# Graph attention, one core: each unit's s1 row spread into PSUM by a TensorE matmul of three bfloat16 parts

## The chip, the cores and the metric

The kernel runs on one core of a Trainium2 chip. The metric is device time in microseconds (us), lower is better; the time before is the median of three runs.

## The reference

One graph attention layer with eight heads, a residual and a layer norm, for 8 graphs of 2048 nodes with 512 features:

```
h  = einsum('bnf,hfo->bhno', x, W)            # 8 heads, 64 features each
s1 = einsum('bhno,ho->bhn', h, a1);  s2 = einsum('bhno,ho->bhn', h, a2)
e  = leaky_relu(s1[..., :, None] + s2[..., None, :], 0.2)
attn = softmax(where(adj > 0, e, -9e15), axis=-1)
out = layernorm(x + concat_heads(attn @ h))
```

## The kernel before

exp(leaky_relu(s1 + s2)) is a product of two factors wherever the sign of s1 + s2 is known, so the attention is worked out as two matmuls with masks of zeros and ones: m_pos holds the edges on which s1_i + s2_j is positive, m_neg the other edges. No exponential of a 2048 x 2048 matrix is taken.

**Work and its units.** A batch is one graph. Its 2048 rows i are cut into KB = 4 blocks of BLK = 512, and each block is done for H = 8 heads, so a batch has UNITS = 32 units (block, head), and the kernel 256. The columns j are cut into JC = 16 chunks of 128, eight to each half ("quad", QUADS = 2).

**A unit on the engines.**
- SyncE (`load_s1`, L261) loads the unit's row of 512 values s1 from DRAM, where `store_s1` put it, into all 128 partitions of `s1_bc`, two buffers deep. Ahead of it, it waits until ScalarE and VectorE have done with the buffer. It also loads adjacency pieces (`load_piece`), transposes them (`turn_piece`), loads x tiles and stores finished blocks, all in one queue, in the order of the program.
- ScalarE (`compare`, L505) copies the row from `s1_bc` into PSUM bank 5 (L510) and then makes 13 of the 16 chunks of `step` (L519), each a steep Relu of s1_i + s2_j that reads the PSUM bank. Around it stand, in its queue, the cuts of adjacency pieces to one byte (`cut_piece`, L487) and the copies of transposed x tiles out of PSUM (`copy_xT`, L493).
- VectorE (L707) makes the other three chunks from `s1_bc` in SBUF, then `m_pos` = step AND mask (`make_pos`, L722) and `m_neg` = m_pos XOR mask (`make_neg`, L731), two instructions each. It waits for ScalarE's half of `step`, and for TensorE to be done with the buffer. Then it takes the finished unit out of PSUM (`take_unit`, L576 to L581). Layer norm and a batch's preparation go between.
- TensorE, for each of four blocks of 128 rows, adds a matmul of a tiny term (L448) and 32 matmuls of 65 columns with m_pos (L454, L455) into one PSUM bank, and then in the same way 32 for m_neg (L475, L476) into another: 260 matmuls to a unit, each with its weight load. Between the two halves it may do a step for the next batch: transpose an x tile (`turn_x`, L368; 16 of the 32 units), sum x (`turn_x_sum`, unit 24), the scores (`sum_scores`, unit 25), `turn_scores` and `mean_h` (unit 27).
- GpSimd divides, adds the residual, sums x, and takes a maximum over partitions once a batch (L862).

**Order.** Every engine runs the same loop over batches. ScalarE and VectorE make the masks of unit u+1 while TensorE multiplies unit u; the masks have two buffers, so VectorE's m_pos of unit u+1 needs the first half of TensorE's unit u-1 to be over. At the head of a batch the hidden features h of all 16 chunks are multiplied (L429, in the three PSUM banks H_BANKS in turn), and VectorE and GpSimd split them into high and low parts (`split_chunk`, L693 to L698): this is called the batch head below, and the 32 units the unit stage. At the end of a batch VectorE prepares the next: `score_maxima` in unit 28, `exponents` in unit 29, `no_edge_start` and `no_edge_part` in unit 30, and `turn_s2` (L665, L666) in unit 31, which ScalarE's first compare of the next batch waits for.

PSUM banks: 0 to 3 hold the sums of two units, 4 the mean and the sum of x, 5 the s1 row, 6 and 7 x tiles and scores; h uses 7, 4 and 6.

Of the kernel before, what the change touches and what calls it, by code (L numbers as in the profile page):

```python
# [60 lines left out]
def gat_kernel(nc, x, adj, W, a1, a2, out):  # L61
# [16 lines left out]
    H_BANKS = (7, 4, 6)  # L78
# [9 lines left out]
    with ExitStack() as ctx:  # L88
# [18 lines left out]
        BANK_MEAN = 4  # L107
        BANK_SUM = 4
        BANK_S1 = 5
        BANK_X = 6  # L110

# [18 lines left out]
        sT = sb("sT", [P, BLK], F32)  # L130
        s_col = sb("s_col", [P, JC, 2 * H], F32)
# [88 lines left out]
        s1_copied = sem("s1_copied")  # L220
# [39 lines left out]
        def _(sp):  # L260
            def load_s1(u, slot):  # L261

                sp.wait_ge(step_act, at(step_act, QUADS * (u - 1)))
                sp.sem_inc(waited[sp.engine], 1)
                sp.wait_ge(step_dve, at(step_dve, u - 1))
                sp.dma_start(s1_bc[slot][:], s1_rows[bass.ds(u, 1), :].rearrange("a n -> (a n)").partition_broadcast(P)
                             ).then_inc(s1_loaded[slot], 16)
# [95 lines left out]
        def _(pe):  # L363
# [8 lines left out]
            def turn_x_sum(n):  # L372
                if type(n) is int:
                    pe.wait_ge(x_added, at(x_added, JC))
                else:
                    pe.wait_ge(x_summed, 16 * JC * n)
                for fc in range(FC):
                    mm = pe.matmul(ps[:, BANK_SUM, fc:fc + 1], x_sum[:, fc * P:(fc + 1) * P], ones[:, 0:1],
                                   start=True, stop=True)
                mm.then_inc(x_sum_turned, 1)  # L380
# [8 lines left out]

            def turn_scores(n):  # L390
                pe.wait_ge(sT_copied, n + 1)
                for t in range(IT):
                    mm = pe.transpose(ps[:, BANK_X + 1, t * P:(t + 1) * P], sT[:, t * P:(t + 1) * P], ident[:])
                mm.then_inc(s_turned, 1)
# [21 lines left out]
            sum_scores(0)  # L416
            mean_h(0)
            turn_scores(0)

            with nc.Fori(0, B, engines=[pe.engine], hint_back_edge=True) as b:  # L420
                for jc in range(JC):
                    if jc == 0:
                        pe.wait_ge(s_col_copied, b + 1)
                    if jc == 1:
                        pe.wait_ge(tiny_step, 6 * b + 1)
                    if jc >= 3:
                        pe.wait_ge(hi_d_made, b * JC + jc - 2)
                    for fc in range(FC):
                        mm = pe.matmul(ps[:, H_BANKS[jc % 3], :], xT[:, fc, jc * P:(jc + 1) * P], W_sb[:, fc, :],  # L429
                                       start=(fc == 0), stop=(fc == FC - 1))  # L430
                    mm.then_inc(h_summed, 1)
                for k in range(KB):
                    g = b * KB + k
                    for h in range(H):
# [22 lines left out]
                        if unit == 0:  # L457
                            pe.wait_ge(lo_made, at(lo_made, 2 * JC * (b + 1)))
                        if unit and unit in TILE_UNIT:
                            t = TILE_UNIT.index(unit)  # L460
                            turn_x(JC * (b + 1) + t, t % 2, (b + 1) * (JC // 2) + t // 2)
# [19 lines left out]
        def _(act):  # L481
# [12 lines left out]

            def copy_scores(n):
                act.wait_ge(sT_summed, n + 1)
                nc.scalar.activation(sT[:], ps[:, BANK_X, :], ACT.Copy).then_inc(sT_copied, 1)

# [6 lines left out]
            def compare(u, h, nth):  # L505
                act.wait_ge(s1_loaded[h % 2], 16 * (nth + 1))
                act.sem_inc(waited[act.engine], 1)

                act.wait_ge(step_act, at(step_act, QUADS * u))
                nc.scalar.activation(ps[:, BANK_S1, :], s1_bc[h % 2][:], ACT.Copy).then_inc(s1_copied, 1)  # L510
                act.wait_ge(s1_copied, u + 1)
                act.sem_inc(waited[act.engine], 1)
                for qd in range(QUADS):
                    act.wait_ge(pos_made, at(pos_made, QUADS * (u - 1) + qd + 1))
                    act.sem_inc(waited[act.engine], 1)
                    for c in range(JQ):
                        if c not in DVE_SLOTS.get(qd, ()):
                            j = qd * JQ + c
                            ins = nc.scalar.activation(chunk(step[qd], c, 0, BLK), ps[:, BANK_S1, :], ACT.Relu,  # L519
                                                       bias=s2_steep[:, j, h:h + 1], scale=STEEP, saturate=False)  # L520
# [10 lines left out]
            exponentials(0)  # L531
            act.wait_ge(s2_turned, 1)
            compare(0, 0, 0)

            with nc.Fori(0, B, engines=[act.engine], hint_back_edge=True) as b:
                for k in range(KB):
                    g = b * KB + k
                    for h in range(H):
# [8 lines left out]
                        if unit == STURN_UNIT:  # L547
                            copy_scores(b + 1)
                        if unit < UNITS - 1:
                            compare(u + 1, (h + 1) % H, g * (H // 2) + (h + 1) // 2)  # L550
                        else:
                            exponentials(b + 1)
                            with act.If(b < B - 1):
                                act.wait_ge(s2_turned, b + 2)
                                act.sem_inc(waited[act.engine], 1)
                                compare(u + 1, 0, (g + 1) * (H // 2))
# [5 lines left out]
        def _(dve):  # L562
# [51 lines left out]
            def score_maxima(n):  # L614
# [7 lines left out]
                V.tensor_reduce(stat[:, H:H + 1], xmax[:], AX.X, ALU.max).then_inc(stat_made, 1)  # L622

# [122 lines left out]
            V.memset(ones_bf[:], 1.0).then_inc(ones_bf_made, 1)  # L746
            V.memset(wa[:], 0.0)
# [27 lines left out]
            score_maxima(0)  # L775
            turn_s2(0)
# [6 lines left out]
            with nc.Fori(0, B, engines=[dve.engine], hint_back_edge=True) as b:  # L783
# [13 lines left out]
                for k in range(KB):  # L797
                    g = b * KB + k
                    for h in range(H):
# [17 lines left out]
                        if unit == STAT_UNIT:  # L817
                            score_maxima(b + 1)
                        if unit == STAT_UNIT + 1:
# [147 lines left out]
```

## Time and profile before

| | |
|---|---|
| median of 3 runs | 3147.84 us (3135.4 to 3163.03) |
| the profiled execution | 3138.42 us |
| its span, first to last instruction | 3136.7 us |
| mean granted TensorE clock | 0.967 of full speed |

The terms below are read in the profiled execution, whose span leaves 1.7 us of its own time outside. It lies 9.4 us (0.3%) under the median of the runs, so a difference in it is carried over to the median as it stands. In the views, PE is TensorE's matmuls, PEld its weight loads, DVE VectorE, ACT ScalarE, POOL GpSimd and SP SyncE. "issue" names idle time in which an engine waited for nothing that the profile shows.

### The profile page before, as it was taken

To read this page: it belongs to the slowest core of one execution; us is meant where nothing else is said; L and a number is where in the kernel's file an instruction comes from. 1 tells how busy PE (TensorE), PEld (TensorE's weight loads), DVE (VectorE), ACT (ScalarE), POOL (GpSimd) and SP (SyncE) were. 2 spreads that over 40 slices of the span, in tenths; PEclk is the share of its full clock that TensorE was granted. 3 is DMA by queue.
4 is the path that set the end of the run, shared out by engine and by line. 5 is a ranking of instruction groups with operands and counts; after the bars stand their busy time and mean duration, and the time that the engine had idled before them with its cause. 6 is when DMAs were issued, how large, how long until landed. Compare 5 with 4: busy or idle time off the path is not lost.

```text
span 3136.7 us, 158793 instructions
## 1 busy us (share of the span) xinstructions
PE 2744.1 (87%) x68636; PEld 2398.0 (76%) x68636; DVE 2522.8 (80%) x3954; ACT 2419.3 (77%) x4029; POOL 827.5 (26%) x1011
## 2 busy tenths in 40 slices
PE   4898889998898898988989889998898888988886
PEld 2498876988678885888858888498884888758886
DVE  4888878887887878888788787888877877788876
ACT  2499973999658996599856998479973989739994
POOL 2522115111341113312142111521215111161211
PEclk9999999999999999999999999999999999999998
DMA  5357643576526655277442765437644556345753
GB/s 162 93 116 161 141 100 100 123 164 131 130 71 136 150 130 136 63 157 157 111 118 70 159 155 122 98 88 165 150 108 115 112 143 156 90 112 115 165 135 94
DMA packets 281338, 392.28 MB, mean 125 GB/s; under 512 B 161856, under 2 KB 161856, under 8 KB 280672
## 3 DMA queue, kind: packets, MB, share of 16 engines
q1 hardware_dynamic: 253536, 315.24, 39.9%
q0 software_dynamic: 27136, 67.12, 12.7%
q8 instruction: 545, 8.93, 1.2%
q14 instruction: 121, 0.99, 0.2%
HBM read 313.52 MB, written 34.14 MB: 111 GB/s over the span
## 4 chain that ended last, share of the span: by engine, by line
PE 67%; issue 13%; DVE 10%; ACT 7%; DMA 1%; SPq 1%; POOL 0%; DVEq 0%; ACTq 0%; POOLq 0%
PE ps L475 14%; PE ps L476 14%; PE ps L455 13%; PE ps L454 13%; PE ps L429 8%; ACT step L519 7%; PE ps L368 2%; DVE m_neg L731 1%; DVE y L603 1%; PE ps L386 1%; PE ps L399 1%; DVE prod L695 1%; PE ps L448 1%; DVE prod_d L698 1%; DVE m_pos L722 1%
## 5 line engine op out<-in xcount | busy, mean ns | idle before, releaser
L519 ACT ACTIVATE step<-ps,s_steep 128x512 fp8e4<-128x512 f32 x3328 | 1954.1, 726 | 289.7 <-DVE m_pos L722 246.9
L455 PE MATMUL ps<-b_lo,m_pos 128*128 128x65 f16 x16384 | 1094.3, 195 | 96.4 <-issue 95.4
L454 PE MATMUL ps<-b_hi,m_pos 128*128 128x65 f16 x16384 | 1093.7, 195 | 54.4 <-issue 36.5
L475 PE MATMUL ps<-d_hi,m_neg 128*128 128x65 f16 x16384 | 1071.9, 195 | 67.0 <-issue 61.2
L455 PEld LDWEIGHTS ps<-b_lo,m_pos 128*128 128x128 fp8e5 x16384 | 1052.3, 98 | 101.3 <-issue 101.0
L475 PEld LDWEIGHTS ps<-d_hi,m_neg 128*128 128x128 fp8e5 x16384 | 1043.6, 99 | 98.5 <-issue 97.9
L476 PE MATMUL ps<-d_lo,m_neg 128*128 128x65 f16 x16384 | 1072.7, 195 | 42.3 <-issue 42.1
L454 PEld LDWEIGHTS ps<-b_hi,m_pos 128*128 128x128 fp8e5 x16384 | 1052.5, 98 | 66.3 <-issue 66.1
L476 PEld LDWEIGHTS ps<-d_lo,m_neg 128*128 128x128 fp8e5 x16384 | 1039.1, 99 | 34.9 <-issue 33.3
L722 DVE TENSOR_TENSOR m_pos<-step,maskT 128x1024 uint32<-128x1024 uint32 x512 | 623.8, 1242 | 163.4 <-ACT step L519 130.6
L731 DVE TENSOR_TENSOR m_neg<-m_pos,maskT 128x1024 uint32<-128x1024 uint32 x512 | 602.8, 1217 | 0.0
L429 PE MATMUL ps<-W_sb,xT 128*128 128x512 f32 x1024 | 464.1, 615 | 61.5 <-DVE prod_d L698 54.7
L871 POOL TENSOR_TENSOR den_scaled<-den_inv,bound 128x4 f32<-128x4 f32 x256 | 74.9, 292 | 1592.0 <-DVE den_inv L581 1533.9
L429 PEld LDWEIGHTS ps<-W_sb,xT 128*128 128x128 f32 x1024 | 200.8, 198 | 319.3 <-issue 240.6
L707 DVE TENSOR_SCALAR step<-s_bc,s_neg 128x512 fp8e5<-128x512 f32 x768 | 391.1, 565 | 12.4 <-DVE s_neg L666 3.6
L487 ACT ACTIVATE adj_cut<-adj_in 128x1024 fp8e4<-128x1024 int32 x264 | 291.1, 1132 | 120.0 <-DMA adj_in<-in_adj 120.0
L576 DVE TENSOR_TENSOR neg_part<-ps,r_row 128x260 f32<-128x260 f32 x256 | 108.8, 425 | 316.3 <-PE ps L476 315.8
L493 ACT ACTIVATE xT<-ps 128x512 f32<-128x512 f32 x144 | 96.9, 673 | 175.8 <-PE ps L368 175.8
L510 ACT ACTIVATE ps<-s_bc 128x512 f32<-128x512 f32 x256 | 174.6, 682 | 71.9 <-DVE s_neg L666 71.4
L876 POOL TENSOR_TENSOR y<-total,den_scaled 128x256 f32<-128x256 f32 x256 | 206.2, 805 | 22.7 <-POOL den_scaled L871 2.3
L448 PE MATMUL ps<-tiny,ones_bf 128*128 128x65 bf16 x1024 | 199.0, 194 | 11.2 <-issue 6.3
L917 POOL TENSOR_TENSOR d_lo<-prod_d,d_hi 128x512 f16<-128x512 f32 x128 | 176.2, 1376 | 9.0
(81 smaller groups left out, 1703.4 us busy)
## 6 DMA issues: line engine op xcount, KB each, us to landing
adj_in<-in_adj SPq DMA_DIRECT2D x266, 512.0 KB, 4.8
s_bc<-s_rows SPq DMA_DIRECT2D x258, 256.0 KB, 3.8
x_in<-in_x SPq DMA_DIRECT2D x144, 256.0 KB, 4.7
x_sum<-in_x POOLq DMA_DIRECT2D x128, 256.0 KB, 4.6
y<-in_x POOLq DMA_DIRECT2D x32, 1024.0 KB, 10.4
out<-y SPq DMA_DIRECT2D x32, 1024.0 KB, 7.4
maskT<-adj_cut SPq DMA_TRANSPOSE x264, 4.3
W_sb<-in_L_gnn_W SPq DMA_DIRECT2D x4, 256.0 KB, 6.8
```

Of the source, the lines that this page charges most:

```text
L429: mm = pe.matmul(ps[:, H_BANKS[jc % 3], :], xT[:, fc, jc * P:(jc + 1) * P], W_sb[:, fc, :], start=(fc == 0), stop=(fc == FC - 1))
L448: pe.matmul(acc, ones_bf[:], tiny[:, h, :], start=True, stop=False)
L454: pe.matmul(acc, mask, b_hi[:, j, h, :], start=False, stop=False)
L455: mm = pe.matmul(acc, mask, b_lo[:, j, h, :], start=False, stop=(j == JC - 1))
L475: pe.matmul(acc, mask, d_hi[:, j, h, :], start=(j == 0), stop=False)
L476: mm = pe.matmul(acc, mask, d_lo[:, j, h, :], start=False, stop=(j == JC - 1))
L487: nc.scalar.activation(adj_cut8[slot][:], adj_in[slot][:], ACT.Relu, scale=STEEP, saturate=False).then_inc(adj_cut, 1)
L519: ins = nc.scalar.activation(chunk(step[qd], c, 0, BLK), ps[:, BANK_S1, :], ACT.Relu, bias=s2_steep[:, j, h:h + 1], scale=STEEP, saturate= ...
L707: ins = V.tensor_scalar(chunk(step[qd], c, 0, BLK).bitcast(FP8_WIDE), s1_bc[hp][:], s2_neg[:, j, h:h + 1], STEP_UP, ALU.is_gt, ALU.mult, s ...
L722: V.tensor_tensor(words(m_pos[hp][:, js, :]), words(step[qd][:]), words(mask[:, js, :]), ALU.bitwise_and).then_inc(pos_made, 1)
L731: V.tensor_tensor(words(m_neg[hp][:, js, :]), words(m_pos[hp][:, js, :]), words(mask[:, js, :]), ALU.bitwise_xor).then_inc(neg_made, 1)
L876: G.tensor_tensor(y[par][:, :, h * O:(h + 1) * O], total[hp][:, :, 0:O], den_scaled[hp][:].unsqueeze(2).to_broadcast([P, IT, O]), ALU.mult ...
```

## The change

ScalarE no longer copies the row from `s1_bc` to PSUM. Once a batch, VectorE cuts the 2048 x 8 values of s1 into three bfloat16 parts (`cut_s1`, four instructions, in unit 28), TensorE transposes them with an identity (`turn_s1`, four matmuls, in unit 29), and ScalarE copies the result to SBUF as `s1_T`, 96 rows of 512 (`copy_s1`, ahead of the compare of unit 31). For each unit TensorE then does one matmul of 512 bfloat16 columns (`spread_s1`), whose stationary operand is one column of a constant matrix `s1_pick`, spread over 128 columns: it picks and adds the unit's three parts into all partitions of a PSUM bank. It is issued two units ahead, between the two halves of a unit, into banks 4 and 5 in turn. ScalarE's compare waits for it. VectorE still reads `s1_bc`, which is loaded as before, but SyncE's load of it no longer waits for ScalarE. To make room, the mean moves from bank 4 to bank 6, the sum of x from bank 4 to bank 7, H_BANKS become (7, 6, 4), `turn_scores(0)` goes ahead of `mean_h(0)`, and some waits are added on TensorE.

```diff
-    H_BANKS = (7, 4, 6)
+    H_BANKS = (7, 6, 4)
+    PARTS = 3
+    S1_ROWS = PARTS * KB * H
...
-        BANK_MEAN = 4
-        BANK_SUM = 4
-        BANK_S1 = 5
+        BANK_S1 = 4
         BANK_X = 6
+        BANK_MEAN = 6
+        BANK_SUM = 7
+        BANK_PARTS = 7
...
+        s1_rest = sb("s1_rest", [P, IT, KB, H], F32)
+        s1_parts = sb("s1_parts", [P, IT, PARTS, KB, H], BF16)
+        s1_T = sb("s1_T", [S1_ROWS, BLK], BF16)
+        s1_pick = sb("s1_pick", [S1_ROWS, KB * H], BF16)
+        ident_bf = sb("ident_bf", [P, P], BF16)
...
             def load_s1(u, slot):
-                sp.wait_ge(step_act, at(step_act, QUADS * (u - 1)))
-                sp.sem_inc(waited[sp.engine], 1)
                 sp.wait_ge(step_dve, at(step_dve, u - 1))
...
                     pe.wait_ge(x_summed, 16 * JC * n)
+                pe.wait_ge(xT_copied, at(xT_copied, JC * (n + 1)))
...
+            def turn_s1(n):
+                pe.wait_ge(s1_cut, 4 * (n + 1))
+                for t in range(IT):
+                    mm = pe.matmul(ps[0:S1_ROWS, BANK_PARTS, t * P:(t + 1) * P],
+                                   s1_parts[:, t, :, :, :].rearrange("p a k h -> p (a k h)"), ident_bf[:], start=True, stop=True)
+                mm.then_inc(s1_turned, 1)
+
+            def spread_s1(unit):
+                pe.matmul(ps[:, BANK_S1 + unit % 2, :], s1_pick[:, unit:unit + 1].to_broadcast([S1_ROWS, P]), s1_T[:],
+                          start=True, stop=True).then_inc(s1_spread, 1)
...
                 pe.wait_ge(sT_copied, n + 1)
+                pe.wait_ge(x_sum_spread, n + 1)
...
             sum_scores(0)
+            turn_scores(0)
             mean_h(0)
-            turn_scores(0)
+            turn_s1(0)
+            pe.wait_ge(s1_T_copied, 1)
+            for unit in range(2):
+                spread_s1(unit)
...
                     if jc == 0:
-                        pe.wait_ge(s_col_copied, b + 1)
+                        pe.wait_ge(s1_T_copied, b + 1)
...
+                    if jc == 2:
+                        pe.wait_ge(step_act, at(step_act, QUADS * (b * UNITS + 1)))
...
+                        if unit == UNITS - 2:
+                            pe.wait_ge(s1_T_copied, b + 2)
+                        spread_s1((unit + 2) % UNITS)
+                        if unit == STAT_UNIT + 1:
+                            turn_s1(b + 1)
...
+            def copy_s1(n):
+                act.wait_ge(s1_turned, n + 1)
+                nc.scalar.activation(s1_T[:], ps[0:S1_ROWS, BANK_PARTS, :], ACT.Copy).then_inc(s1_T_copied, 1)
...
-            def compare(u, h, nth):
-                act.wait_ge(s1_loaded[h % 2], 16 * (nth + 1))
-                act.sem_inc(waited[act.engine], 1)
-                act.wait_ge(step_act, at(step_act, QUADS * u))
-                nc.scalar.activation(ps[:, BANK_S1, :], s1_bc[h % 2][:], ACT.Copy).then_inc(s1_copied, 1)
-                act.wait_ge(s1_copied, u + 1)
+            def compare(u, h):
+                act.wait_ge(s1_spread, u + 1)
...
-                            ins = nc.scalar.activation(chunk(step[qd], c, 0, BLK), ps[:, BANK_S1, :], ACT.Relu,
+                            ins = nc.scalar.activation(chunk(step[qd], c, 0, BLK), ps[:, BANK_S1 + h % 2, :], ACT.Relu,
...
+                        if unit == STAT_UNIT + 2:
+                            copy_s1(b + 1)
...
+            def cut_s1(n):
+                s1 = s_col[:].rearrange("p (k t) s -> p t k s", t=IT)[:, :, :, 0:H]
+                V.tensor_copy(s1_parts[:, :, 0, :, :], s1).then_inc(s1_cut, 1)
+                dve.wait_ge(s1_cut, 4 * n + 1)
+                V.tensor_tensor(s1_rest[:], s1, s1_parts[:, :, 0, :, :], ALU.subtract).then_inc(s1_cut, 1)
+                dve.wait_ge(s1_cut, 4 * n + 2)
+                V.tensor_copy(s1_parts[:, :, 1, :, :], s1_rest[:]).then_inc(s1_cut, 1)
+                dve.wait_ge(s1_cut, 4 * n + 3)
+                V.tensor_tensor(s1_parts[:, :, 2, :, :], s1_rest[:], s1_parts[:, :, 1, :, :], ALU.subtract).then_inc(s1_cut, 1)
...
             score_maxima(0)
+            cut_s1(0)
...
                             score_maxima(b + 1)
+                            cut_s1(b + 1)
```

Left out are the semaphores, three VectorE instructions that make `s1_pick` once at the start, and the changed calls of `compare`.

## Rows read from the trace of the kernel before

**Rows 1.** The page: busy share by engine, and the chain that ended last, by engine

```profile
PE 2744.1 (87%) x68636; PEld 2398.0 (76%) x68636; DVE 2522.8 (80%) x3954; ACT 2419.3 (77%) x4029; POOL 827.5 (26%) x1011
...
PE 67%; issue 13%; DVE 10%; ACT 7%; DMA 1%; SPq 1%; POOL 0%; DVEq 0%; ACTq 0%; POOLq 0%
```

**Rows 2.** Windows, the 8 unit stages: length, busy us (instructions) by engine, clock, DMA

```profile
141.80:450.40 308.60, 278.87 (x8432) 270.96 (x8432) 252.27 (x390) 267.99 (x452) 59.73 (x88) 0.98 0.57 126
...
2415.60:2733.60 318.00, 281.12 (x8432) 271.88 (x8432) 254.90 (x394) 268.74 (x453) 59.43 (x88) 0.98 0.54 126
...
sum 2512.10, PE 2244.12 PEld 2174.85 DVE 2031.97 ACT 2143.23 POOL 474.96; mean PE 280.52 PEld 271.86 DVE 254.00 ACT 267.90 POOL 59.37
```

**Rows 3.** Windows, what lies between: start, 7 batch heads (one stands), end; sum

```profile
0.00:141.80 141.80, 90.75 (x256) 43.52 (x257) 90.49 (x150) 52.36 (x80) 60.65 (x58) 0.95 0.49 134
...
1208.80:1275.10 66.30, 58.50 (x140) 25.71 (x137) 56.74 (x96) 32.35 (x50) 41.22 (x35) 0.95 0.45 112
...
sum 624.60, PE 499.96 PEld 223.10 DVE 490.81 ACT 276.09 POOL 352.53; mean PE 55.55 PEld 24.79 DVE 54.53 ACT 30.68 POOL 39.17
```

**Rows 4.** Waits, whole execution: us in total, times, longest us

```profile
DVE neg_part L576 <- PE ps L476: 315.8, 154, 8.2
...
ACT step L519 <- DVE m_pos L722: 246.9, 101, 15.8
...
PE ps L455 <- issue: 95.4, 75, 3.4
...
PE ps L475 <- issue: 61.2, 43, 2.8
...
PE ps L476 <- issue: 42.1, 32, 3.2
...
PE ps L454 <- issue: 36.5, 41, 2.3
...
PE ps L448 <- issue: 6.3, 7, 1.5
...
PE ps L475 <- DVE m_neg L731: 5.5, 2, 3.0
```

**Rows 5.** Instruction fetch: the page's queue; windows between two gaps, PE alone; the gap

```profile
q8 instruction: 545, 8.93, 1.2%
...
2115.97:2121.07 5.10, 4.09 (x127) 1.00 0.94 253
2121.07:2128.34 7.27, 4.12 (x127) 1.00 1.08 194
...
2128.35 0.20 PE L455 MATMUL ps<-b_lo,m_pos 128*128 128x65 f16 x1 [3.13 <-issue]
```

**Rows 6.** ScalarE's timeline in a unit: start us, us, line [idle before it]

```profile
1104.44 1.15 ACT L487 ACTIVATE adj_cut<-adj_in 128x1024 fp8e4<-128x1024 int32 x1
1105.38 0.69 ACT L510 ACTIVATE ps<-s_bc 128x512 f32<-128x512 f32 x1
1106.35 7.63 ACT L519 ACTIVATE step<-ps,s_steep 128x512 fp8e4<-128x512 f32 x13 [0.28 <-ACT ps L510]
```

**Rows 7.** Chain of the window 780 to 1180: wide float32 matmuls, one batch

```profile
782.76 3.44 PE ps L399 x8
```

**Rows 8.** Timeline of VectorE and ScalarE at the end of a batch

```profile
1183.42 0.42 DVE L616 COPY s_col<-ps 128x256 f32<-128x256 f32 x1
...
1191.83 0.29 DVE L627 TENSOR_TENSOR s_rel<-s_col,stat_all 128x128 f32<-128x128 f32 x1 [0.32 <-POOL stat_all L862]
...
1197.24 1.23 DVE L722 TENSOR_TENSOR m_pos<-step,maskT 128x1024 uint32<-128x1024 uint32 x1 [0.36 <-ACT step L519]
...
1207.52 0.22 DVE L666 TENSOR_SCALAR s_neg<-s_col 128x128 f32<-128x128 f32 x1
...
1208.02 0.60 ACT L510 ACTIVATE ps<-s_bc 128x512 f32<-128x512 f32 x1 [10.22 <-DVE s_neg L666]
1208.89 7.63 ACT L519 ACTIVATE step<-ps,s_steep 128x512 fp8e4<-128x512 f32 x13 [0.27 <-ACT ps L510]
...
1216.56 1.23 DVE L722 TENSOR_TENSOR m_pos<-step,maskT 128x1024 uint32<-128x1024 uint32 x1 [2.83 <-ACT step L519]
```

**Rows 9.** Timelines of TensorE and VectorE at the start

```profile
63.98 3.70 PE L399 MATMUL ps<-W_sb,prod 128*128 128x512 f32 x8
...
68.23 0.42 DVE L616 COPY s_col<-ps 128x256 f32<-128x256 f32 x1 [6.53 <-PE ps L393]
```

More of the change, by code:

```diff
@@ L219, in gat_kernel @@
         r_row_made = sem("r_row_made")
-        s1_copied = sem("s1_copied")
+        s1_cut = sem("s1_cut")
+        s1_turned = sem("s1_turned")
+        s1_T_copied = sem("s1_T_copied")
+        s1_spread = sem("s1_spread")
+        pick_step = sem("pick_step")
         step_act = sem("step_act", free=QUADS)
@@ L531, in _ @@
             exponentials(0)
+            copy_s1(0)
             act.wait_ge(s2_turned, 1)
-            compare(0, 0, 0)
+            compare(0, 0)
             with nc.Fori(0, B, engines=[act.engine], hint_back_edge=True) as b:
@@ L548, in _ @@
                             copy_scores(b + 1)
+                        if unit == STAT_UNIT + 2:
+                            copy_s1(b + 1)
                         if unit < UNITS - 1:
-                            compare(u + 1, (h + 1) % H, g * (H // 2) + (h + 1) // 2)
+                            compare(u + 1, (h + 1) % H)
                         else:
@@ L555, in _ @@
                                 act.sem_inc(waited[act.engine], 1)
-                                compare(u + 1, 0, (g + 1) * (H // 2))
+                                compare(u + 1, 0)
                         for i in late:
@@ L746, in _ @@
             V.memset(ones_bf[:], 1.0).then_inc(ones_bf_made, 1)
+            dve.wait_ge(consts_made, 1)
+            V.tensor_copy(ident_bf[:], ident[:]).then_inc(pick_step, 1)
+            dve.wait_ge(pick_step, 1)
+            V.tensor_tensor(s1_pick[:], ident_bf[0:S1_ROWS, 0:KB * H], ident_bf[0:S1_ROWS, KB * H:2 * KB * H], ALU.add
+                            ).then_inc(pick_step, 1)
+            dve.wait_ge(pick_step, 2)
+            V.tensor_tensor(s1_pick[:], s1_pick[:], ident_bf[0:S1_ROWS, 2 * KB * H:3 * KB * H], ALU.add).then_inc(pick_step, 1)
             V.memset(wa[:], 0.0)
```

## The prediction

> **What bounds the kernel now.** I read the busy shares first: TensorE 87%, VectorE 80% and ScalarE 77% are close, and a share alone decides nothing; the chain that ended last gives TensorE 67%, "issue" 13% and ScalarE 7% [rows 1]. Then the windows. The 8 unit stages, where the change puts its per-unit work, take 2512.1 of the 3136.7 us of span; TensorE is busy for 280.5 us of each stage's mean 314.0 and ScalarE for 267.9 [rows 2]. Start, batch heads and end take the other 624.6 [rows 3].
>
> The waits decide who bounds the unit stage. The reader should look for TensorE waiting for masks. That would stand as a wait of L448 or L475 on VectorE, and the only such row that carries anything is 5.5 us in 2 waits. What TensorE does idle for is "issue": 95.4 + 61.2 + 42.1 + 36.5 + 6.3 = 241.5 us in 198 gaps of 1.2 us in the mean, inside runs of matmuls as well as between them. VectorE in turn waits 315.8 us for TensorE's finished units, and ScalarE 246.9 us for buffers that VectorE frees [rows 4]. So TensorE bounds the units, and ScalarE, whose copy goes, is a follower there.
>
> The gaps have a place. The instruction queue moved 8.93 MB in 545 packets, and 68,636 matmuls over 545 are 126; between the ends of two gaps lie exactly 127 matmuls, twice [rows 1, 5]. The gaps are instruction blocks that arrive late: 4.1 us of work, then a wait of up to 3.13 us [rows 5].
>
> **ScalarE's copy goes.** From the start of the copy to the first step is 1106.35 - 1105.38 = 0.97 us, so 256 x 0.97 = 248 us leave ScalarE [rows 6]. In the unit stage I price this at nothing: TensorE never waits for it. At each batch head it is on the path: VectorE's L666 ends at 1207.74, the copy starts at 1208.02, the steps at 1208.89, and both halves of m_pos wait for them [rows 8]. That is -0.87 us in each of 7 heads.
>
> **The spread comes to TensorE.** It is one matmul of 512 bfloat16 columns per unit, which the trace doesn't show. The nearest wide row is float32: 8 records of 512 columns in 3.44 us, 0.43 each, two records to a matmul [rows 7]. That is the upper end. From below: 127 matmuls of 65 columns keep TensorE busy for 4.09 us, 0.032 each [rows 5]; by columns that is 0.25 for 512, with each one's fixed part in it, and half a float32 record, as for half the bytes, is 0.22. I take 0.22, the plain width, and keep 0.43 for the range; a price below 0 for the matmul alone is excluded, as TensorE works in order. 
> Who pays 0.22? In a batch's last units TensorE isn't the end of the path: from 1183.42 on VectorE works through to L666 at 1207.52 with two waits, 0.32 and 0.36 [rows 8], and the next head hangs on it. So the spreads of units 28 to 31 are hidden in 7 of 8 batches: 7 x 28 + 32 = 228 spreads count, 228 x 0.22 = 50.2 us.
>
> Some of it is given back. A block that comes late comes at a time that the DMA sets; a matmul executed before it fills part of the gap. 198 gaps over 545 blocks is 36%, and their mean of 1.2 us is far over 0.22, so the spread in such a block is free: 50.2 x 0.64 = 32.1 us. The Trainium skill, "Runtime: NRT & Kernel Launch", section Instruction fetch mechanics, says the next block is fetched while the current one executes, and that crossing costs little and is mostly hidden. The trace disagrees on the second with 241.5 us; by the page alone nothing would be absorbed, which is the first rival.
>
> **ScalarE's new wait.** compare(u+2) now waits for a matmul that TensorE issues after the first half of unit u; the cuts of adjacency pieces and the x copies behind it in ScalarE's queue wait too, and SyncE's transposes behind these. The steps take 7.63 us [rows 6] and the second m_pos 1.23 [rows 8], so the mask of unit u+2 is there about 9.2 us after that half. TensorE needs it three halves of 130 matmuls later, 3 x 4.1 = 12.3 us [rows 5]. The cover is 3 us; without it each unit would lose what is missing. This also stops compare(2) from running in the batch head, where ScalarE is mostly idle; the same 3 us cover it. TensorE's other new waits (x_sum after the last x copy, jc 2 after the first compare, jc 0 after s1_T) come after work that is done earlier: 0.
>
> **Once a batch.** cut_s1 puts four dependent VectorE instructions in unit 28, on the path just named. The like rows are 0.22 to 0.42 each [rows 8]: 1.3 us, of which the two waits take 0.68 back. With -0.87 this leaves -0.25 x 7 = -1.8 us; ends: -6 (cut hidden) to +4 (waits stay). turn_s1 and copy_s1 (one ScalarE copy of 0.69, as that of L510, where a unit's own copy stood) are hidden: 0.
>
> **SyncE.** It still moves 256 KB per unit. load_s1 is no longer held until ScalarE has finished a unit, so the queue behind it (x loads, transposes, pieces) runs some us earlier. Price 0; its ends are below.
>
> **Start.** turn_scores(0) no longer stands behind mean_h(0), 3.70 us [rows 9], and s_col, the maximum and the exponents follow it; copy_s1(0) and a spread take some 0.7 back over the removed copy. I take -2.7, ends -3.7 and +1.
>
> **Sum.** 32.1 - 1.8 - 2.7 = +27.6 us on 3138.4, so 3166. Carried to the median: 3147.8 + 27.6 = 3175.5, +0.9%.
>
> **Rivals.**
> - *Nothing is absorbed*: blocks come later just as TensorE does, because the request itself is tied to what TensorE has consumed. 50.2 - 4.5 = +46, 3194. For it: gaps recur after each block of a run, as at 2121 and 2128 [rows 5]. Against: DMA share is 0.94 to 1.08 there against 0.54 to 0.57 over a stage [rows 2, 5], so the DMA's load sets the time.
> - *The wide matmul is dear*, near a float32 record of 0.43: 228 x 0.43 = 98, less 36% is 63, less 4.5 is +58, 3206; unabsorbed +94.
> - *The other side: late blocks come sooner.* load_s1 no longer falls together with the transposes and piece loads that ScalarE's cuts release, so the instruction blocks find the DMA engines less crowded in units 8 to 31. The unit stages now range from 308.6 to 318.0 us with equal work (TensorE busy 278.9 and 281.1) [rows 2], so gaps do vary that much. If all ran like the shortest, 2512.1 - 8 x 308.6 = -43, net -16, 3132. It decides once the 241.5 us of gaps shrink by more than 27.6, 11%. Against: the loads are as large as before, and VectorE's part of compare, for which load_s1 still waits, ends within some us of ScalarE's.
> - *It does nothing*: the spreads fall wholly into gaps, and only heads and start change: -4.5, 3143. That ScalarE's relief speeds up the units is no more than the 5.5 us of mask waits.
>
> **How the numbers follow.** My forecast, 3175, has 0.46, with a range of its own of 3160 to 3190; nothing absorbed 0.18; dear 0.12; sooner 0.16; nothing 0.08. The range of 3134 to 3210 reaches from the one end to the other and leaves out the unabsorbed dear case and the tail of the sooner one. About 1% (31 us) is what a measurement of this kernel can tell from no change. Slower by over 1%: 0.18 + 0.12 + the upper third of the forecast, 0.14 = 0.44. Faster by over 1% needs the gaps to shrink by over 59 us: 0.08. Within 1%: 0.48.
>
> **What would show it.** Right: L510 gone; in the unit stage ScalarE's idle time up by about what it saved; the spread's row with 228 to 256 x 0.2 of pitch; TensorE's stage some 4 us longer; "issue" gaps on TensorE down from 241.5 to about 225; heads within 1 us of 66.3. Wrong: waits of L448 on m_pos over 20 us (the new wait isn't covered), "issue" changed by more than 30 us either way, or a spread that holds up the next matmul by 0.4 us.

## The result, and the profile after

The changed kernel takes 3163.64 us (median of 20 executions, 3142.74 to 3174.72) against 3148.13 for the kernel before on the same chip (20 executions): ratio 1.0049, interval 1.0026 to 1.0072, +15.5 us. The forecast was +27.6, with a range from 3134 to 3210. The profiled execution took 3150.68, of which 3149.0 are span, at a mean granted clock of 0.975; that of before had a span of 3136.7 at 0.967. Ratios, and means over executions, are taken from the fast ones of a kernel's executions alone, medians from all.

The page of the changed kernel: busy shares, the chain that ended last (engines, then lines), and its groups of the steps and of the spread.

```profile
PE 2777.2 (88%) x68930; PEld 2418.0 (77%) x68930; DVE 2527.9 (80%) x3993; ACT 2288.0 (73%) x3782; POOL 833.8 (26%) x1011
...
PE 75%; issue 12%; DVE 9%; ACT 1%; POOL 0%; DVEq 0%; ACTq 0%; POOLq 0%
...
L557 ACT ACTIVATE step<-ps,s_steep 128x512 fp8e4<-128x512 f32 x3328 | 1962.2, 760 | 671.8 <-PE ps L413 478.8
```

ScalarE is busy for 131 us less, where 248 us had been counted from each copy's start to the first step. It left the chain (7% to 1%), and TensorE's share rose from 67% to 75% [rows 1].

The windows of the changed kernel over the 8 unit stages (two stand, with the sum) and over start and 7 heads (start, two heads, sum); columns as in [rows 2].

```profile
138.60:454.70 316.10, 285.11 (x8468) 274.17 (x8468) 254.01 (x395) 263.00 (x440) 60.26 (x88) 0.98 0.55 124
...
1664.30:1988.70 324.40, 289.27 (x8468) 277.63 (x8468) 255.49 (x397) 262.88 (x440) 61.28 (x88) 0.97 0.54 123
...
sum 2550.40, PE 2285.84 PEld 2198.12 DVE 2037.69 ACT 2094.40 POOL 481.08; mean PE 285.73 PEld 274.76 DVE 254.71 ACT 261.80 POOL 60.14
```
```profile
0.00:138.60 138.60, 91.35 (x264) 44.22 (x265) 91.85 (x156) 43.46 (x64) 60.67 (x58) 0.96 0.51 137
...
829.90:895.40 65.50, 58.74 (x139) 25.71 (x136) 56.39 (x96) 22.20 (x33) 41.22 (x35) 0.95 0.44 113
1216.80:1278.50 61.70, 56.03 (x137) 24.61 (x134) 55.66 (x94) 21.07 (x31) 41.28 (x35) 1.00 0.47 120
...
sum 576.00, PE 491.23 PEld 219.82 DVE 484.27 ACT 193.58 POOL 349.46; mean PE 61.40 PEld 27.48 DVE 60.53 ACT 24.20 POOL 43.68
```

Beside [rows 2, 3] this splits the span's +12.3: unit stages +38.3 (2550.4 - 2512.1), start -3.2 (138.6 - 141.8), the 7 heads -22.9 (437.4 - 460.3), end +0.1. Forecast were +32.1, -2.7 and -1.8. The reader should see two terms of opposite sign, where the total alone shows one small one. Six of the heads take 60.8 to 63.5 us at a clock of 0.97 to 1.00 and one 65.5 at 0.95; before, they took 64.4 to 66.6 at 0.92 to 0.95.

The waits of the changed kernel, whole execution: total us, times, longest.

```profile
ACT step L557 <- PE ps L413: 478.8, 105, 39.4
DVE neg_part L617 <- PE ps L515: 404.8, 188, 8.5
...
PE ps L487 <- issue: 99.5, 59, 4.1
...
PE ps L488 <- issue: 76.2, 65, 3.0
...
PE ps L515 <- issue: 46.6, 36, 4.2
...
PE ps L514 <- issue: 16.6, 16, 2.4
...
PE ps L481 <- issue: 4.1, 5, 2.1
```

L481, L487, L488, L514 and L515 are what L448, L454, L455, L475 and L476 were. The first row is the new wait: ScalarE idles 478.8 us for spreads, and no row has TensorE waiting for m_pos. TensorE's "issue" in the units is 99.5 + 76.2 + 46.6 + 16.6 + 4.1 = 243.0, against 241.5 in [rows 4]. TensorE has 41.7 us more of busy time in the stages (2285.8 - 2244.1) and nearly as much idle time as before (264.6 against 268.0).

The spread in the timeline of TensorE (start, us, line), changed kernel:

```profile
577.21 0.19 PE L488 MATMUL ps<-b_lo,m_pos 128*128 128x65 f16 x1
577.24 0.38 PE L413 MATMUL ps<-s_T,s_pick 96*128 96x512 bf16 x1
577.46 0.60 PE L380 MATMUL ps<-ident,x_in 128*128 128x128 f32 x4
```

The record lasts 0.38, but the next matmul starts 577.46 - 577.24 = 0.22 after it: the pitch is what counts, and it is the one forecast.

A head, before and after: TensorE's timelines of both (rows in brackets name the idle time), then the windows of TensorE's first 8 records after that idle time, before and after. A float32 matmul leaves two records, so a chunk of h is 4 matmuls and 8 records.

```profile
1208.78 0.19 PE L476 MATMUL ps<-d_lo,m_neg 128*128 128x65 f16 x1
1209.07 10.56 PE L429 MATMUL ps<-W_sb,xT 128*128 128x512 f32 x24
1226.87 8.66 PE L429 MATMUL ps<-W_sb,xT 128*128 128x512 f32 x14 [7.24 <-DVE prod_d L698]
```
```profile
1216.74 0.19 PE L515 MATMUL ps<-d_lo,m_neg 128*128 128x65 f16 x1
1219.49 10.56 PE L462 MATMUL ps<-W_sb,xT 128*128 128x512 f32 x24 [2.56 <-issue]
1232.73 7.56 PE L462 MATMUL ps<-W_sb,xT 128*128 128x512 f32 x17 [2.67 <-DVE prod_d L749]
```
```profile
1226.80:1233.10 6.30, 6.23 (x9) 2.75 (x10) 6.30 (x12) 1.90 (x3) 4.14 (x5) 0.61 1.13 174
```
```profile
1232.70:1236.20 3.50, 3.47 (x8) 1.63 (x9) 3.50 (x6) 0.94 (x1) 3.31 (x3) 1.00 1.04 206
```

Before, TensorE does chunks 0 to 2 at once (24 records), idles 7.24 us until VectorE frees a bank, and does chunk 3 at a granted clock of 0.61 over the window, mostly at the lower of its two levels, 1.2 GHz: the eight records of a chunk take 6.3 us. After, an "issue" gap of 2.56 us at the loop's back edge moves chunk 0 later, the idle time for VectorE is 2.67, the clock stays at 2.4 GHz, and the same eight take 3.5 us. In this head the gap costs nothing, as it comes out of the idle time. In three of the seven the clock is at its lower level for 3.4 us from about the gap's end, and chunks 0 to 2 take 1.5 to 1.7 us longer; these are the heads of 63.3, 61.4 and 63.5 us.

Over the 7 heads, from the start of chunk 3 to that of chunk 4 took 5.9 us in the mean before and 3.9 after, -13.5 us in all; chunk 3 itself starts 17.6 us after the stage's end before and 16.3 after, -9.4 in all. Together these are the heads' -22.9. Of the second term, 0.7 us in each head is the removed copy: VectorE's first m_pos starts 4.77 us after s_neg before and 4.03 after.

### The profile page after: what moved, and what is told of

It reads as the page before. It is cut to its first block, busy times and chain, and to the rows that moved or that the text cites. A ratio compares the mean times of both kernels' runs of the same rounds, so it can differ in the third digit from the quotient of the medians.

```text
span 3149.0 us, 158151 instructions
## 1 busy us (share of the span) xinstructions
PE 2777.2 (88%) x68930; PEld 2418.0 (77%) x68930; DVE 2527.9 (80%) x3993; ACT 2288.0 (73%) x3782; POOL 833.8 (26%) x1011
## 4 chain that ended last, share of the span: by engine, by line
PE 75%; issue 12%; DVE 9%; ACT 1%; POOL 0%; DVEq 0%; ACTq 0%; POOLq 0%
PE ps L487 15%; PE ps L488 15%; PE ps L515 15%; PE ps L514 15%; PE ps L462 8%; PE ps L380 2%; PE ps L413 2%; DVE m_neg L782 1%; ACT step L557 1%; DVE prod L746 1%; PE ps L481 1%; PE ps L399 1%; PE ps L426 1%; DVE prod_d L749 1%; DVE y L644 1%
## 5 line engine op out<-in xcount | busy, mean ns | idle before, releaser
L557 ACT ACTIVATE step<-ps,s_steep 128x512 fp8e4<-128x512 f32 x3328 | 1962.2, 760 | 671.8 <-PE ps L413 478.8
L487 PE MATMUL ps<-b_hi,m_pos 128*128 128x65 f16 x16384 | 1101.8, 195 | 117.0 <-issue 99.5
L488 PE MATMUL ps<-b_lo,m_pos 128*128 128x65 f16 x16384 | 1102.3, 195 | 76.9 <-issue 76.2
L488 PEld LDWEIGHTS ps<-b_lo,m_pos 128*128 128x128 fp8e5 x16384 | 1061.8, 99 | 118.4 <-issue 118.2
L487 PEld LDWEIGHTS ps<-b_hi,m_pos 128*128 128x128 fp8e5 x16384 | 1061.7, 99 | 88.7 <-issue 88.1
L515 PE MATMUL ps<-d_lo,m_neg 128*128 128x65 f16 x16384 | 1051.8, 194 | 47.3 <-issue 46.6
L514 PEld LDWEIGHTS ps<-d_hi,m_neg 128*128 128x128 fp8e5 x16384 | 1030.4, 98 | 60.1 <-issue 59.8
L514 PE MATMUL ps<-d_hi,m_neg 128*128 128x65 f16 x16384 | 1052.4, 194 | 17.4 <-issue 16.6
L515 PEld LDWEIGHTS ps<-d_lo,m_neg 128*128 128x128 fp8e5 x16384 | 1021.0, 98 | 37.1 <-issue 22.8
L931 POOL TENSOR_TENSOR den_scaled<-den_inv,bound 128x4 f32<-128x4 f32 x256 | 86.8, 339 | 1599.9 <-DVE den_inv L622 1537.9
L462 PE MATMUL ps<-W_sb,xT 128*128 128x512 f32 x1024 | 455.0, 606 | 37.3 <-DVE prod_d L749 19.7
L481 PE MATMUL ps<-tiny,ones_bf 128*128 128x65 bf16 x1024 | 199.7, 195 | 9.3 <-issue 4.1
L975 POOL TENSOR_TENSOR b_lo<-prod,b_hi 128x512 f16<-128x512 f32 x128 | 144.1, 1126 | 95.1 <-DVE prod L746 92.2
L909 POOL DMA_DIRECT2D x_sum<-in_x x128 | 118.1, 923 | 89.5 <-DMA x_sum<-in_x 82.7
```

The source lines that it names most:

```text
L481: pe.matmul(acc, ones_bf[:], tiny[:, h, :], start=True, stop=False)
L487: pe.matmul(acc, mask, b_hi[:, j, h, :], start=False, stop=False)
L488: mm = pe.matmul(acc, mask, b_lo[:, j, h, :], start=False, stop=(j == JC - 1))
L514: pe.matmul(acc, mask, d_hi[:, j, h, :], start=(j == 0), stop=False)
L515: mm = pe.matmul(acc, mask, d_lo[:, j, h, :], start=False, stop=(j == JC - 1))
```

## The experiments

All ratios are against the kernel before on the same chip, with their 95% intervals. "Stages" is the sum over the 8 unit stages, "issue" TensorE's in the units as above, each from the one profiled execution. One such sum is good to some 30 us: kernels whose unit code is the same gave 2550.4 and 2546.2, 2511.9 and 2482.7, and 2513.6 and 2480.6 (the last pair is `b_warm` and `b_warm_turn`), each in two separate measurements. So where the ratio and the stages disagree, the ratio counts. "Clock deficit" is span times (1 - granted clock), the mean over the executions of a kernel; it doesn't tell in which stretch the clock was low.

**Is it the matmul?** On one chip; the kernel before had 3153.49 us there.

`a_triple`: two more spreads in each unit, 512 x 0.22 = 113 us of work.

```
                         spread_s1((unit + 2) % UNITS)
+                        for _ in range(2):
+                            pe.matmul(ps[:, BANK_S1 + unit % 2, :], s1_pick[:, unit:unit + 1].to_broadcast([S1_ROWS, P]), s1_T[:], start=True, stop=True)
```

> The changed kernel with two more spread matmuls ahead of each, into the same bank. Adds 256 x 0.44 = 113 us of TensorE work in the unit stages. Theory (a matmul ahead of a late instruction block is free; 36% of the blocks are late): the unit stages grow by 65 to 85 us and the gaps on TensorE shrink by 25 or more. Rival (the fetch follows TensorE, so nothing is absorbed): they grow by 105 to 115 us.

Ratio 1.0213 [1.0174, 1.0253], 3220.35 us. The windows' sum over its stages:

```profile
sum 2614.20, PE 2396.57 PEld 2249.68 DVE 2038.04 ACT 2094.27 POOL 478.81; mean PE 299.57 PEld 281.21 DVE 254.76 ACT 261.78 POOL 59.85
```

Stages +63.8 over the changed kernel (2614.2 - 2550.4), while TensorE's busy time there rises by 110.7; "issue" falls from 243.0 to 197.4. So 42% of the added work went into gaps, near the 36% of the forecast's absorption. The stages grew by a little less than the 65 to 85 us expected, and far less than the 105 of "nothing absorbed".

`a_narrow`: the loop's spreads write 8 columns only, so that most of ScalarE's s1 rows stay those of an earlier unit.

```
-            pe.matmul(ps[:, BANK_S1 + unit % 2, :], ..., s1_T[:], ...)
+            pe.matmul(ps[:, BANK_S1 + unit % 2, 0:n], ..., s1_T[:, 0:n], ...)      # n = 8 in the loop
```

> The changed kernel with each spread inside the loop only 8 columns wide instead of 512; the rest of the bank keeps what stood there, so the masks are of stale rows. Every wait and instruction stays. Theory (the price is the width of 0.22 us, of which late instruction blocks give a quarter to a third back): the unit stages fall from 2550 us to that of the kernel before, 2512 (2500 to 2525). Rival (the whole 0.22 is paid and ScalarE's relief gives 18 us back): they fall by 49 us to about 2500 or under.

Ratio 1.0009 [0.9984, 1.0034], 3159.22 us. Stages 2556.4: TensorE's busy time fell by 21.8 us (2285.8 to 2264.1), and "issue" rose by 27 (243.0 to 270.2). The busy time fell by less than the 49 us that 256 x 0.19 of columns make, as the stages' granted clock was lower here (0.96 to 0.99 against 0.97 to 0.98). Both expectations missed: a spread almost without columns doesn't bring the stages back to 2512. Between `a_narrow` and `a_triple`, on the same chip, lie 228 x 0.19 + 113 = 156 us of matmul work and 61 us of time, 39%. By that share the forecast's 50.2 us of spreads cost about 20, an estimate. Something else would have to make up the rest of +38.3.

`a_copy_back`: the spreads stay; ScalarE's copy of the loaded row and its wait come back, into the same bank, and so does SyncE's wait for ScalarE ahead of load_s1.

```
             def load_s1(u, slot):
+                sp.wait_ge(step_act, at(step_act, QUADS * (u - 1)))
...
+                act.wait_ge(s1_loaded[h % 2], 16 * (nth + 1))
...
+                act.wait_ge(step_act, at(step_act, QUADS * u))
+                nc.scalar.activation(ps[:, BANK_S1 + h % 2, :], s1_bc[h % 2][:], ACT.Copy).then_inc(s1_copied, 1)
+                act.wait_ge(s1_copied, u + 1)
```

> The changed kernel with ScalarE's copy of s1_bc into the PSUM bank put back ahead of each compare (after the spread has written the bank), and SyncE's wait for it. TensorE's work is that of the changed kernel. Theory (TensorE bounds the units, ScalarE's relief is worth nothing there): the 8 unit stages stay at 2550 us (within 15), each batch head is 0.9 us longer, 6 us in all. Rival (ScalarE's 0.97 us per unit was worth part of what the spread costs, and that is why the loss is less than 32 us): the unit stages grow by 15 to 40 us.

Ratio 0.9977 [0.9954, 1.0001], 3145.68 us. Its stages:

```profile
sum 2511.90, PE 2287.54 PEld 2197.54 DVE 2039.01 ACT 2218.34 POOL 476.32; mean PE 285.94 PEld 274.69 DVE 254.88 ACT 277.29 POOL 59.54
```

I expected 2550 and that theory fell, and so did its rival, longer stages. TensorE has all of the change's work (busy 2287.5 against 2285.8) and the stages are 38.5 us shorter; "issue" went from 243.0 to 200.6, which is all of it. The heads gave 25.8 us back: they took 463.2 against 437.4, with the lower clock in chunk 3 in all seven although the gap at the back edge was there (15.8 us in 7). Work added to ScalarE and waits added to it and to SyncE made the kernel faster. So the change's loss is in what it takes away, the prediction's "price 0".

**Which of the two?** Another chip; before, 3129.66 us.

`a_sp_wait`: the changed kernel with SyncE's wait alone.

```
             def load_s1(u, slot):
+                sp.wait_ge(step_act, at(step_act, QUADS * (u - 1)))
```

> The changed kernel with one wait put back: SyncE's load_s1 waits for ScalarE's steps again, as in the kernel before. ScalarE's copy stays away. Theory 1 (the order and time of SyncE's transfers cost the unit stages of the changed kernel some 40 us, as the late instruction blocks meet them; the spreads themselves nearly fit into the gaps): the 8 unit stages are at 2500 to 2520 us against 2550, the gaps over 0.25 us on TensorE at about 255, the time about 15 us under the kernel before. Theory 2 (it was ScalarE's earlier pace, which releases the adjacency pieces sooner): the stages stay at 2540 to 2560.

Ratio 1.0091 [1.006, 1.0122]; stages 2553.3, "issue" 244.1: no gain. (The changed kernel itself didn't run on this chip; on two others it has 1.0049 and 1.0079.)

`a_act_slow`: ScalarE copies its bank onto itself ahead of each compare and waits for that; SyncE isn't touched.

```
+                act.wait_ge(step_act, at(step_act, QUADS * u))
+                nc.scalar.activation(ps[:, BANK_S1 + h % 2, :], ps[:, BANK_S1 + h % 2, :], ACT.Copy).then_inc(waste_made, 1)
+                act.wait_ge(waste_made, u + 1)
```

> The changed kernel with ScalarE held back: ahead of each compare it copies the PSUM bank onto itself (0.7 us and the wait for it), nothing else is changed, SyncE's wait stays away. Theory 1 (SyncE's wait matters, ScalarE's pace doesn't): stages stay at 2540 to 2560 us. Theory 2 (ScalarE's pace matters): stages at 2500 to 2520, like the run with copy and wait put back.

Ratio 1.0082 [1.0056, 1.0107]; stages 2533.5, "issue" 233.0: part of the way in the stages, nothing in the ratio. Neither alone does it. What `a_copy_back` has beyond the two is ScalarE's wait for the loaded row. Its waits show no row in which ScalarE idles for that load, but no run takes this wait alone, nor SyncE's wait together with the slower ScalarE.

**Is it real, or where the code lies?** A third chip; before, 3127.44 us. Here the changed kernel itself ran again, with the copy-back kernel beside it (`a_copy_back2`, the same code as `a_copy_back`).

> The changed kernel itself once more, on the same chip as the three that follow, since the two groups of runs so far were on two chips on which the kernel before took 3153 and 3130 us. Theory (the loss is a property of the change): ratio to the kernel before 1.003 to 1.009. Mean granted clock 0.970 or higher against 0.966 of the kernel before, that is 12 us or more less lost to the low clock.

> The kernel with ScalarE's copy and SyncE's wait put back, once more. Theory (TensorE bounds the units; the copy costs only in the heads): ratio to the changed kernel 1.000 to 1.004, ratio to the kernel before about 1.008. Rival (the first run, 0.9977 of the kernel before and 22 us under the changed kernel, was the effect and not the chip: the spread is nearly free, and what costs is that ScalarE and SyncE run at another time): ratio to the kernel before 0.995 to 1.000, gaps on TensorE in the unit stages at 255 us against 296 to 301.

`a_again`: 1.0079 [1.0046, 1.0112], 3152.43 us. `a_copy_back2`: 0.9994 [0.9959, 1.0029], 3117.43 us. The stages of the two, and their "issue" rows:

```profile
sum 2546.20, PE 2294.52 PEld 2206.68 DVE 2033.22 ACT 2086.86 POOL 478.91; mean PE 286.82 PEld 275.84 DVE 254.15 ACT 260.86 POOL 59.86
```
```profile
sum 2482.70, PE 2279.02 PEld 2189.58 DVE 2037.12 ACT 2212.22 POOL 477.64; mean PE 284.88 PEld 273.70 DVE 254.64 ACT 276.53 POOL 59.70
```
```profile
PE ps L487 <- issue: 81.7, 51, 3.4
PE ps L488 <- issue: 77.2, 60, 2.9
PE ps L515 <- issue: 39.3, 32, 4.5
PE ps L514 <- issue: 22.3, 25, 2.7
```
```profile
PE ps L491 <- issue: 66.4, 72, 3.4
PE ps L490 <- issue: 47.9, 42, 4.4
PE ps L517 <- issue: 32.1, 30, 3.0
PE ps L518 <- issue: 24.6, 23, 2.6
```

The ratios differ by 0.84%, about 27 us, where `a_copy_back` against the changed kernel's first measurement had 0.72%; the two profiled stages differ by 63.5, of which 53.5 are "issue". The mean spans of the executions lie 32.8 us apart and those of the two profiled ones 52.9, so the profiles overstate it. The clock isn't it: the deficits are 90.3 and 87.0 us.

`b_shift`: the kernel before with 32 one-column matmuls (64 instructions, a quarter of a block) in the head's idle time, so that every later block boundary lies elsewhere.

```
+                    if jc == 3:
+                        pe.wait_ge(unit_read, at(unit_read, b * UNITS - 1))
+                        for _ in range(32):
+                            pe.matmul(ps[:, 0, 300:301], ones_bf[:], ones_bf[:, 0:1], start=True, stop=True)
```

> The kernel before with 32 matmuls of one column (64 instructions, 1 us in each batch head while TensorE waits for VectorE anyway), which write an unused column of PSUM. The instructions behind them fall a quarter of an instruction block later. Theory (moving the code alone moves the late blocks, and so the time, by some tenths of a per cent): the sum of gaps in the unit stages differs by 10 us or more from the kernel before, the time by up to 0.5% either way. Rival (only added work counts): stages at 2512 us within 8, time within 0.2%.

Ratio 1.0025 [0.9997, 1.0053]; stages 2519.7, "issue" 256.8. The units' gaps moved by 15 us, which is within what two profiles of one kernel differ by (243.0 and 224.8 for the changed kernel), so that placement moves them isn't shown. It did bring the back-edge gap, 21.6 us in 7 heads, that the changed kernel has too (17.6), and with it shorter heads: 446.9 us against 460.3, of which chunk 3 makes 14.5 (3.8 us in the mean against 5.9). So the kernel before, with its ScalarE and SyncE as they were, gets the clock's half of the heads' gain from where its code lies, or from the 32 small matmuls in the idle time, which this run can't tell apart. In the time nothing clear comes of it.

**Is it the clock in the heads?** `b_warm` (first chip) and `b_warm2` (second) are the kernel before, with chunk 2 of the head done twice or three times, 3.4 or 6.9 us of work in the idle time; `a_sp_warm` (second chip) is `a_sp_wait` with chunk 2 done twice.

```
-                    for fc in range(FC):
+                    for fc in list(range(FC)) * (2 if jc == 2 else 1):      # b_warm2: 3
```

> The kernel before with the matmuls of chunk jc 2 of h done twice in each batch head (same result, same bank), which fills 3.4 of the 7 us that TensorE idles there. Theory (the heads of the changed kernel are 3 to 5 us shorter because TensorE's idle time there fell under what brings its clock down to 1.2 GHz, and the first chunks after it then run at 2.4 GHz): no low clock right after the idle time, each of the 7 heads about 3 us shorter (66 to 63), 20 us in all, unit stages unchanged. Rival (the shorter heads come from the copy that went and from the spreads hidden at the end of a batch): heads unchanged at 66.

> The kernel before with the matmuls of chunk jc 2 of h done three times in each batch head (same result), so that TensorE works until 17.6 us after the head's start, where chunk 3 may start at 17.9. Theory (what is saved in the head is the clock that doesn't fall): no stretch at 1.2 GHz in the heads, chunk 4 starts 3.4 us after chunk 3 in all of them, heads at 63 instead of 66, 20 us in all, time 0.6% under the kernel before. Rival (the profile of the run with two repeats, heads 62 to 67, shows that idle time isn't what sets it): heads stay at 66 and the time within 0.3% of the kernel before.

> The changed kernel with SyncE's wait put back and chunk jc 2 done twice in each batch head: the version that the two theories point to. If both hold: stages at 2500 to 2520 us, heads at 61 to 62, 3148 - 15 - 25 = about 3110 us, 1.2% under the kernel before. If SyncE's wait isn't the cause: about 3150. If the fill doesn't hold the clock: about 3135.

`b_warm`: 0.994 [0.9907, 0.9973], deficit 106.6 to 87.8 us, mean span -18.6. Its one profiled execution had only one short head (62.4) and the others 65.2 to 67.2: 460.5 us in all against 460.3, as the rival said. The idle time ahead of chunk 3 had fallen to 3.1 to 4.2 us in these six, and the clock fell all the same. `b_warm2`: 0.9981 [0.9954, 1.0008], deficit 103.1 to 79.7, but all heads 66.5 to 68.3. It has a back-edge gap of 3.4 us in each head, which `b_warm` hasn't, and with it the filling was too long: chunk 3 starts 20.8 to 22.6 us after the stage's end. `a_sp_warm`: 1.0047 against 1.0091 of `a_sp_wait`, with intervals that overlap, deficit 99.7 to 82.2; 1.2% under the kernel before was expected, and it is slower. Its heads take 451.7 against 451.6: chunk 3 runs 9 us faster in all and starts 9 us later. A filling of one chunk goes with 0.4 to 0.6% and with a smaller deficit, but no profile shows shorter heads.

`b_warm_turn`: `b_warm` with the change's order at the start, turn_scores(0) ahead of mean_h(0).

> The kernel before with chunk jc 2 done twice in each head, and turn_scores(0) ahead of mean_h(0) at the start as in the change. Theory: the clock in the heads gives 18 us (0.6%), as in the run with the fill alone, and the start 3 us: ratio to the kernel before 0.993, mean clock 0.972. If the fill's gain was chance: ratio 0.999.

Ratio 0.9923 [0.989, 0.9956], 3104.53 us; start 139.1 against 141.8, though starts in the old order were 139.8 to 142.7. Its stages, then start and heads:

```profile
sum 2480.60, PE 2238.29 PEld 2169.70 DVE 2028.13 ACT 2136.63 POOL 473.19; mean PE 279.79 PEld 271.21 DVE 253.52 ACT 267.08 POOL 59.15
```
```profile
sum 599.20, PE 517.90 PEld 231.68 DVE 487.68 ACT 279.56 POOL 351.13; mean PE 64.74 PEld 28.96 DVE 60.96 ACT 34.94 POOL 43.89
```

The heads are 599.2 - 139.1 = 460.1 us, as before (460.3). What is shorter in this profile is the stages, by 31.5 us. So the time is what was expected and the place isn't: that the clock in the heads gives the gain isn't shown, and that the repeated matmuls moved the code of the units is a rival that no run here tests. The kernel has the lowest ratio here, and on its chip it is 0.8% under the kernel before and 1.5% under the changed one.

## Why the forecast held, and where its steps did not

- **TensorE bounds the units, ScalarE's relief is worth nothing**: right, and short of the truth. No mask wait came, the new wait is covered (478.8 us of ScalarE's idle time, none of TensorE's); but the relief had a price, below.
- **The spread's pitch, 0.22 us**: right to the hundredth; the dear rival (0.43) is out.
- **A part is absorbed**: right in kind. 64% was to be paid; `a_triple` paid 58% in the stages, the pair `a_narrow` and `a_triple` 39% in the time. "Nothing absorbed" is out. "It does nothing" is out for the change as a whole (the interval starts at 1.0026), but for the spreads alone it isn't: with copy and wait put back, they are all there and the ratios are 0.9977 and 0.9994.
- **Spreads of units 28 to 31 are hidden**: in part. They lengthen the stage, and the head gives it back: s_neg is made 1.7 us before TensorE's last unit ends before the change, 2.3 after (1.5 in `a_again`, so this is one profile's word).
- **SyncE and ScalarE earlier, price 0**: the step that failed. Putting back both shortened the profiled stages by 38.5 and 63.5 us and the time by 0.72 and 0.84%, 23 and 27 us, with the spreads in place. The total was forecast well and its make-up wasn't: the stage term of 32.1 stands against 38.3 measured, but it was to be spreads alone. How the 38.3 divides stays open. By the share of `a_narrow` and `a_triple` some 20 are spreads and the rest the relief, an estimate; by the copy-back kernels, whose stages are at or under the 2512.1 of before, nearly all of it is the relief. The forecast had 225 for "issue"; the changed kernel's two profiles have 243.0 and 224.8, so this sign can't be read.
- **Heads -1.8**: too small by 21. Its own terms were right: from s_col to s_neg takes 24.7 us in place of 24.3, and the m_pos after it comes 0.74 sooner, -0.3 a head where -0.25 was forecast. But 13.5 us came from the clock in chunk 3, which the sum didn't look at though [rows 3] show 0.95 in a head. `a_again` has less of it, heads of 448.1 us, 7.9 of the 12.2 by chunk 3. That gain isn't in the change's mechanism; the back-edge gap and `b_shift` suggest that it goes with where the code lies, which isn't shown. It stands against the failed step, and so the total came out 12 us from the forecast (+15.5 against +27.6), which is in part luck.
- **Start -2.7**: -3.2 measured, and -2.7 by `b_warm_turn` alone, within 3 us of spread between starts of the old order. Two small sums don't come out of their own terms: 3.70 less 0.7 is -3.0, and the upper end of the heads, 7 x (1.3 - 0.87), is +3 and not +4. Neither moves the forecast by more than 0.3 us.

What the earlier ScalarE and SyncE do to the blocks I can argue, not show. Each row pair is SyncE's issue of load_s1 for unit 20 and TensorE's first matmul of unit 18, batch 1, with the late block that follows: before, after, and `a_copy_back2`, from their timelines.

```profile
682.76 0.33 SPq L266 DMA_DIRECT2D s_bc<-s_rows  x1
...
686.83 0.19 PE L448 MATMUL ps<-tiny,ones_bf 128*128 128x65 bf16 x1
...
688.97 0.20 PE L455 MATMUL ps<-b_lo,m_pos 128*128 128x65 f16 x1 [0.87 <-issue]
```
```profile
681.07 0.33 SPq L278 DMA_DIRECT2D s_bc<-s_rows  x1
...
686.88 0.19 PE L481 MATMUL ps<-tiny,ones_bf 128*128 128x65 bf16 x1
...
691.43 0.19 PE L487 MATMUL ps<-b_hi,m_pos 128*128 128x65 f16 x1 [4.06 <-issue]
```
```profile
687.12 0.33 SPq L281 DMA_DIRECT2D s_bc<-s_rows  x1
...
688.20 0.20 PE L484 MATMUL ps<-tiny,ones_bf 128*128 128x65 bf16 x1 [1.45 <-DVE m_pos L782]
...
689.07 0.19 PE L490 MATMUL ps<-b_hi,m_pos 128*128 128x65 f16 x1 [0.36 <-issue]
```

The load leads by 4.1, 5.8 and 1.1 us, and the gap is 0.87, 4.06 and 0.36. As a mean over units 9 to 26 of all batches, load_s1 leads by this much, beside the sum of the stages:

```
kernel          lead us   stages us
before           5.2       2512.1   (no spreads)
a_copy_back2     3.5       2482.7
a_copy_back      4.4       2511.9
a_sp_wait        6.0       2553.3
a_act_slow       6.3       2533.5
a_again          6.7       2546.2
after            6.6       2550.4
a_narrow         6.7       2556.4
a_sp_warm        5.7       2538.9
a_triple         6.7       2614.2   (two more spreads)
b_warm_turn      4.6       2480.6   (no spreads)
b_warm2          5.0       2494.0   (no spreads)
b_shift          5.2       2519.7   (no spreads)
b_warm           5.2       2513.6   (no spreads)
```

It would also tell why neither half of the copy-back worked: with SyncE's wait alone ScalarE finishes early and the lead only falls to 6.0; with a slower ScalarE alone SyncE waits for VectorE and it stays at 6.3. `a_sp_wait` isn't in its order, though, and piece loads, transposes and x loads moved along with load_s1. Nor does the table say which way it works: a TensorE held up by late blocks starts its unit later, and that alone makes the load lead by more. No run moves load_s1 and nothing else. Which transfer the late blocks meet wasn't tried and stays open.

## What to carry to other kernels

Relieving an engine that isn't the bound needn't be free of cost: ask what it and the queues behind it will now start earlier, and put a range on that instead of a 0. Where two errors may cancel, look at the parts: split the span by stage, and test the forecast on the stages' sums as well as on the total, from more than one profile, as they scatter by 30 us here. And look at the clock in each stage: an idle time of TensorE ahead of serial work can cost twice, as itself and by the clock after it (7.24 us, then 6.3 in place of 3.5). Filling it with repeated matmuls is a change of one line, but look whether the stretch gets shorter: here the time fell by 0.4 to 0.6% and the heads did not.

## What the runs showed of the hardware

- After 7.24 us of idle time TensorE did 8 float32 records in 6.3 us; after 2.67 us in 3.5. The lower level held for 6.8 or 10.2 us in the heads of before. The length of the idle time alone doesn't decide: with 3.3 us of it a head of `a_copy_back` fell to the lower level, and one of `b_warm_turn` with 3.9 didn't.
- A loop's back edge cost less than 0.4 us before and in `b_warm`, 2.5 in the mean after (17.6 over 7), 3.1 in `b_shift` (21.6) and 3.4 in `b_warm2` (23.5), which differs from `b_warm` by 4 matmuls in the body. The Trainium skill, "Runtime: NRT & Kernel Launch", section Instruction fetch mechanics, says that a taken branch to code outside the window held forces a fetch. That the cost changes when the code is moved these runs show; that it is this fetch no run here isolates.
- A matmul whose stationary operand is one column repeated by a step of 0 has a weight load of 97 ns, as the mask's weight loads beside it (97 to 98), and a pitch of 0.22 us at 512 bfloat16 columns.
- Chips differ by more than the change: the kernel before had medians of 3153.49, 3129.66 and 3127.44 us on three of them.
